# Turning x and k by VectorE blocks over DRAM in a Performer layer's keys pass, with one block of value sums per group

## The reference

```python
xn = _layernorm(x)
q, k, v = xn @ wq, xn @ wk, xn @ wv            # 16 heads of 32
def phi(u):                                    # u scaled by 32 ** -0.25, omega 128 x 32
    proj = u @ omega.T
    return exp(proj - 0.5 * sum(u * u) - max(proj)) / sqrt(128) + 1e-6
kv = einsum('bhsm,bhsk->bhmk', phi(k), v)      # sum over the 1024 rows of a batch
z  = sum(phi(k), axis=rows)
```

## Time and profile before

| | |
|---|---|
| median of 3 runs | 3278.48 us (3276.39 to 3280.28) |
| profiled execution, its own time | 3278.06 us |
| its span, first to last instruction | 3276.3 us |
| PE / PEld / DVE / ACT / POOL busy | 98% / 86% / 69% / 51% / 33% |
| mean granted TensorE clock | 0.992 |
| DMA queue of the kernel | 438.46 MB, 42.2% of 16 engines |

### The profile page before, as it was taken

One profiled execution on the slowest core, in us unless ns is written; L12 is line 12 of the kernel. 1 busy time (PEld: TensorE's weight loads), 2 busy tenths in 40 slices (PEclk: granted clock), 3 DMA queues, 4 the chain that ended last, 5 costly groups with the idle time before them and its releaser, 6 DMA issues.

```text
span 3276.3 us, 73388 instructions
## 1 busy us (share of the span) xinstructions
PE 3213.0 (98%) x28265; PEld 2818.2 (86%) x28265; DVE 2259.3 (69%) x4742; ACT 1656.6 (51%) x3552; POOL 1087.9 (33%) x857
## 2 busy tenths in 40 slices
PE   7999999999899999999999999999999999999998
PEld 6777777777777778787878789999999999999998
DVE  6777777776666666666666666666666766676666
ACT  5666666666545545455545454434444444444443
POOL 3554555554456656565656430000000000000000
PEclk9999999999899999999999999999999999999999
DMA  3222222222444444535444574544554454444443
GB/s 123 94 85 78 101 88 88 95 89 78 119 122 137 128 134 119 149 104 154 118 135 128 158 233 159 166 163 162 168 163 161 154 168 164 151 154 162 163 163 134
DMA packets 314123, 443.16 MB, mean 135 GB/s; under 512 B 162608, under 2 KB 187696, under 8 KB 313776
## 3 DMA queue, kind: packets, MB, share of 16 engines
q1 hardware_dynamic: 313776, 438.46, 42.2%
HBM read 309.28 MB, written 129.11 MB: 134 GB/s over the span
## 4 chain that ended last, share of the span: by engine, by line
PE 45%; POOL 9%; DVE 7%; issue 4%; DMA 4%; ACT 3%; SPq 2%; DVEq 0%; ACTq 0%; POOLq 0%
PE ffn_hidden L189 21%; PE attend_gated L189 13%; PE ffn_result L189 5%; POOL shared_y L1172 3%; PE attend_feat L1335 2%; POOL shared_y L1170 2%; POOL attend_oT_lo L1154 2%; DMA ffn_r_in<-r_d 2%; PE attend_num L1373 2%; PE attend_turn L1373 2%; DVE ffn_yb L1794 2%; POOL attend_ka_lo L1150 1%; ACT ffn_ht_hi L1697 1%; POOL shared_mix_lo L1146 1%; SPq L142 1%
## 5 line engine op out<-in xcount | busy, mean ns | idle before, releaser
L189 PE MATMUL ffn_hidden<-ffn_yT_hi,ffn_wa_hi 128*128 128x256 f32 x2048 | 573.2, 280 | 7.3 <-DVE ffn_wa_lo L1715 4.7
L189 PE MATMUL ffn_hidden<-ffn_yT_lo,ffn_wa_hi 128*128 128x256 f32 x2048 | 574.1, 280 | 0.0
L189 PE MATMUL ffn_hidden<-ffn_yT_hi,ffn_wa_lo 128*128 128x256 f32 x2048 | 572.8, 280 | 0.0
L334 POOL TENSOR_TENSOR ffn_n_rstd<-ffn_n_base,ffn_n_power 128x2 f32<-128x2 f32 x32 | 27.5, 859 | 1277.3 <-DVE ffn_n_negmean L329 1277.3
L189 PEld LDWEIGHTS ffn_hidden<-ffn_yT_hi,ffn_wa_hi 128*128 128x128 f32 x2048 | 386.1, 189 | 8.8 <-DVE ffn_wa_lo L1715 5.6
L189 PEld LDWEIGHTS ffn_hidden<-ffn_yT_hi,ffn_wa_lo 128*128 128x128 f32 x2048 | 386.3, 189 | 0.0
L189 PEld LDWEIGHTS ffn_hidden<-ffn_yT_lo,ffn_wa_hi 128*128 128x128 f32 x2048 | 385.9, 188 | 0.2
L1697 ACT ACTIVATE ffn_ht_hi<-ffn_hs 128x512 fp32r<-128x512 f32 x248 | 156.3, 630 | 431.6 <-DVE ffn_hs L1744 431.6
L1748 DVE TENSOR_TENSOR ffn_ht_lo<-ffn_hs,ffn_ht_hi 128x512 fp32r<-128x512 f32 x248 | 173.6, 700 | 218.7 <-ACT ffn_ht_hi L1697 218.7
L703 ACT ACTIVATE keys_e<-keys_feat,keys_below 128x128 f32<-128x128 f32 x1024 | 282.6, 412 | 55.2 <-DVE keys_below L768 55.2
L638 POOL TENSOR_TENSOR keys_z_sum<-keys_z_sum,keys_e 128x512 f32<-128x512 f32 x192 | 243.7, 1286 | 190.1 <-ACT keys_e L703 190.0
(11 more groups left out here) (281 smaller groups left out, 9406.8 us busy)
## 6 DMA issues: line engine op xcount, KB each, us to landing
ffn_tq<-part_d SPq DMA_DIRECT2D x248, 512.0 KB, 5.3
keys_xin<-in_L_attn_x_dram SPq DMA_DIRECT2D x32, 512.0 KB, 4.2
xn_d<-keys_xn SPq DMA_DIRECT2D x32, 512.0 KB, 2.8
xT_d<-keys_xT_whole SPq DMA_DIRECT2D x32, 512.0 KB, 2.6
u_d<-keys_uq_turned SPq DMA_DIRECT2D x32, 512.0 KB, 2.9
shared_xTf<-xT_d SPq DMA_DIRECT2D x32, 512.0 KB, 6.5
r_d<-shared_gate SPq DMA_DIRECT2D x32, 512.0 KB, 2.8
attend_o<-rden_d SPq DMA_DIRECT2D x128, 128.0 KB, 2.7
```

The costliest lines, as they stand in the source:

```text
L189: last = pe.matmul(out, stationary[a], moving[b], start=start and n == 0, stop=stop and n == len(TERMS) - 1)
```

## The change

Rows are now dealt to partitions in pairs (row 2p + t on partition p), so that a turned group can be put together in row order. xn and k are turned by VectorE in 32x32 blocks, stored to DRAM (`xt_d`, `kt_d`) and loaded back by `load_turned`, four DMAs that put each block where it belongs; xT is loaded whole, rounded and split from SBUF, and stored from there, without GpSimd. Only group 0 is still turned by TensorE (`first`). Products of all three kinds, and the features, read every second column of what was turned (`tile_of`). The floor is no longer added to the exponentials: VectorE sums v over the rows (`v_sum`), and the fold adds the floor times that sum in a further product. The value sums of a group are one job of 64 matmul instructions into one bank (`sums`), added by one VectorE instruction, and it stands right before the second feature block. The pipeline is one group deeper for x: `stats`, `norm` and `turn_x` run three groups ahead, `split` two. Banks, waits, the head and the end lists follow from that.

```diff
-        PE_BODY = [("kv", 0, -1), ("turn_x", 1, 1), ("kv", 1, -1), ("proj", 0, 0), ("k", 0, 1), ("k", 1, 1),
-                   ("kv", 2, -1), ("q", 0, 1), ("proj", 1, 0), ("turn_k", 0, 1), ("kv", 3, -1), ("q", 1, 1),
-                   ("turn_k", 1, 1), ("v", 0, 1), ("fold", 0, -1), ("turn_x", 0, 2), ("v", 1, 1)]
+        PE_BODY = [("k", 0, 1), ("k", 1, 1), ("proj", 0, 0), ("q", 0, 1), ("q", 1, 1), ("v", 0, 1), ("kv", 0, -1),
+                   ("proj", 1, 0), ("fold", 0, -1), ("v", 1, 1)]
+        DVE_BODY = [("v_sum", 1, 0), ("sq_q", 0, 0), ("sq_q", 1, 0), ("turn_k", 0, 1), ("turn_k", 1, 1),
+                    ("top", 0, 0), ("sq", 0, 1), ("stats", 0, 3), ("split", 0, 2), ("split", 1, 2),
+                    ("kv", 0, -1), ("top", 1, 0), ("sq", 1, 1), ("v_sum", 0, 1), ("turn_q", 0, 1), ("turn_q", 1, 1), ("turn_x", 0, 3)]
+        ACT_BODY = [("k", 0, 1), ("k", 1, 1), ("exp", 0, 0), ("exp", 1, 0), ("exp", 2, 0), ("exp", 3, 0),
+                    ("split", 0, 2), ("split", 1, 2), ("q", 0, 1), ("q", 1, 1), ("norm", 0, 3), ("v_out", 0, 1),
+                    ("fold", 0, -1), ("exp", 4, 0), ("exp", 5, 0), ("exp", 6, 0), ("exp", 7, 0), ("v_out", 1, 1)]
+        POOL_BODY = [("z", 0, 0), ("z", 1, 0), ("stats", 0, 3), ("z", 2, 0), ("z", 3, 0), ("z", 4, 0), ("z", 5, 0),
+                     ("z", 6, 0), ("z", 7, 0)]
+        SP_BODY = [("u", 0, 0), ("xt_in", 0, 2), ("kt_out", 0, 1), ("kt_in", 0, 1), ("whole", 0, 2), ("sums", 0, -1),
+                   ("x", 0, 4), ("xn", 0, 3), ("xt_out", 0, 3)]
...
+                if job == "xt_in":
+                    sp.wait_ge(xt_stored, 16 * g + 16)
+                    wait(sp, x_split, 2 * (g - 1))
+                    if g > 1:
+                        wait_alone(sp, xT_stored, 16 * (g - 1), sp_passed)
+                    load_turned(sp, xT_whole[g % 2], xt_d[g], xt_loaded[g % 2])
+                if job == "kt_in":
+                    wait_alone(sp, kt_stored, 16 * g + 16, sp_passed)
+                    for j in range(HC):
+                        wait(sp, feat[j].full, TG * (g - 1))
+                    load_turned(sp, kT[g % 2], kt_d[g], k_loaded[g % 2])
...
+                if job == "split":
+                    act.wait_ge(xt_loaded[g % 2], 64 * (g // 2 + 1))
+                    for t in range(TG):
                         wait(act, v_full[t], g - 1)
+                    act.activation(xT[g % 2].hi[:, 2 * n:2 * n + 2, :], xT_whole[g % 2][:, 2 * n:2 * n + 2, :], ACT.Copy)\
+                        .then_inc(xT_hi, 1)
...
+                if job == "split":
+                    dve.wait_ge(xT_hi, 2 * g + n + 1)
+                    dve.tensor_tensor(xT[g % 2].lo[:, 2 * n:2 * n + 2, :], xT_whole[g % 2][:, 2 * n:2 * n + 2, :],
+                                      f32(xT[g % 2].hi[:, 2 * n:2 * n + 2, :]), ALU.subtract).then_inc(x_split, 1)
                 if job == "turn_x":
+                    wait(dve, xt_stored, 16 * g)
+                    for t in range(TG):
+                        dve.wait_ge(xn_ready, TG * g + t + 1)
+                        dve.transpose(xn_turned[:, :, :, t], xn[:, t, :].rearrange("p (b k) -> p b k", k=KD)).then_inc(x_turned, 1)
...
-                if job == "pk":
-                    t, c = n // NC, n % NC
-                    wait(dve, kv_full, NC * (g - 1) + c + 1)
-                    dve.wait_ge(e_ready[t], NC * g + c + 1)
-                    dve.tensor_scalar(pk[t][:, c, :], e[t][:, c, :], FLOOR, None, ALU.add).then_inc(pk_ready[t], 1)
                 if job == "kv":
+                    total = kv_sum[b % 2][:, :, :].rearrange("p c m -> p (c m)")
...
+                    dve.wait_ge(kv_full, g + 1)
+                    wait(dve, kv_added, g)
                     if i == 0:
+                        dve.tensor_copy(total, sums[:, :]).then_inc(kv_added, 1)
                     else:
+                        dve.tensor_tensor(total, sums[:, :], total, ALU.add).then_inc(kv_added, 1)
...
                 if job == "kv":
+                    wait(pe, kv_added, g)
+                    wait(pe, fold_out, pieces_before(g))
...
+                    for c in range(NC):
+                        for t in range(TG):
+                            for j in range(HC):
+                                h = c * HC + j
+                                last = pe.matmul(sums[rows(j), c * M:(c + 1) * M], v[g % 2][:, t, h * KD:(h + 1) * KD],
+                                                 e[t][:, c, j * M:(j + 1) * M], start=c == 0 and t == 0,
+                                                 stop=c == NC - 1 and t == TG - 1)
                     last.then_inc(kv_full, 1)
                 if job == "fold":
...
+                    if g < G - 1:
+                        pe.wait_ge(kv_added, g + 1)
+                        wait(pe, fold_out, pieces_before(g))
...
+                        pe.matmul(out[:, :, 0:KD], floor[:, :],
+                                  v_sum[b % 2][:, c * M:(c + 1) * M].rearrange("p (h k) -> p h k", k=KD),
+                                  start=False, stop=True)
```

More of the change, by code:

```diff
@@ L336, in invert @@
         pool.tensor_tensor(self.shift[:, :], self.negmean[:, :], self.rstd[:, :], ALU.mult).then_inc(self.ready, 1)
[L339 to L347, removed]
@@ L362 @@
[L362 to L369, removed]
+PE_KEYS_END = (("keys", "k", 0, -1), ("keys", "k", 1, -1), ("keys", "proj", 0, -2), ("keys", "q", 0, -1),
+               ("keys", "q", 1, -1), ("keys", "v", 0, -1), ("keys", "kv", 0, -3), ("keys", "proj", 1, -2),
+               ("keys", "fold", 0, -3), ("keys", "v", 1, -1), ("next", "turn", 0, 0), ("next", "turn", 1, 0),
+               ("keys", "kv", 0, -2), ("keys", "proj", 0, -1), ("keys", "fold", 0, -2), ("next", "turn", 2, 0),
+               ("next", "turn", 3, 0), ("next", "turn", 4, 0), ("keys", "proj", 1, -1), ("next", "turn", 5, 0),
+               ("keys", "kv", 0, -1), ("keys", "fold", 0, -1))
@@ new lines @@
+DVE_KEYS_END = (("keys", "v_sum", 1, -2), ("keys", "sq_q", 0, -2), ("keys", "sq_q", 1, -2), ("keys", "turn_k", 0, -1),
+                ("keys", "turn_k", 1, -1), ("keys", "top", 0, -2), ("keys", "sq", 0, -1), ("keys", "kv", 0, -3),
+                ("keys", "top", 1, -2), ("keys", "sq", 1, -1), ("keys", "v_sum", 0, -1), ("keys", "turn_q", 0, -1),
+                ("keys", "turn_q", 1, -1), ("next", "first", 0, 0), ("next", "lo", 0, 0), ("keys", "v_sum", 1, -1),
+                ("next", "lo", 1, 0), ("keys", "kv", 0, -2), ("keys", "sq_q", 0, -1), ("keys", "sq_q", 1, -1),
+                ("keys", "top", 0, -1), ("next", "lo", 2, 0), ("next", "lo", 3, 0), ("next", "lo", 4, 0),
+                ("keys", "top", 1, -1), ("next", "lo", 5, 0), ("next", "mixed", 0, 0), ("keys", "kv", 0, -1),
+                ("next", "lo", 6, 0), ("next", "lo", 7, 0))
@@ L375 @@
[L375 to L381, removed]
[2 rows of a table added]
@@ new lines @@
+                 ("next", "diff", 0, 0), ("next", "mix", 0, 0))
+SP_KEYS_END = (("next", "w", 0, 0), ("next", "w", 1, 0), ("next", "w", 2, 0), ("keys", "u", 0, -2),
+               ("keys", "kt_out", 0, -1), ("keys", "kt_in", 0, -1), ("keys", "sums", 0, -3), ("keys", "u", 0, -1),
+               ("next", "x", 0, 0), ("next", "mu", 0, 0), ("next", "w", 3, 0), ("next", "w", 4, 0),
+               ("keys", "sums", 0, -2), ("next", "w", 5, 0), ("next", "w", 6, 0), ("next", "q", 0, 0),
+               ("next", "w", 7, 0), ("keys", "sums", 0, -1))
@@ L406, in keys_pass @@
         xT = [Pair(mem, ctx, f"xT{n}", [P, NC, GT]) for n in range(2)]
-        xT_whole = sb("xT_whole", [P, NC, GT])
+        xT_whole = [sb(f"xT_whole{n}", [P, NC, GT]) for n in range(2)]
+        xn_turned = sb("xn_turned", [P, H, KD, TG])
+        uk_turned = sb("uk_turned", [P, H, KD, TG])
         uq = sb("uq", [P, TG, D])
@@ L413, in keys_pass @@
         squares = [sb(f"squares{t}", [P, D]) for t in range(TG)]
-        kT = sb("kT", [P, NC, GT])
+        kT = [sb(f"kT{n}", [P, NC, GT]) for n in range(2)]
         v = [sb(f"v_parts{n}", [P, TG, D]) for n in range(2)]
@@ L419, in keys_pass @@
         e = [sb(f"e{t}", [P, NC, HC * M]) for t in range(TG)]
-        pk = [sb(f"pk{t}", [P, NC, HC * M]) for t in range(TG)]
         kv_sum = [sb(f"kv_sum{n}", [P, NC, M]) for n in range(2)]
+        v_sum = [sb(f"v_sum{n}", [P, D]) for n in range(2)]
         z_sum = sb("z_sum", [P, NC, HC * M])
@@ L424, in keys_pass @@
         fold_z = sb("fold_z", [P, M])
+        floor = sb("floor", [P, M])
         kv_out = sb("kv_out", [P, H, KW])
@@ L492, in pieces_before, with first_bank @@
             return max(0, g - GB + 1)
-        def kv_bank(g, n):
-            return (ring[0], ring[2])[n % 2] if g >= G - 2 else (ring[0], ring[2], ring[1], ring[0])[n]
         def fold_bank(g, c):
-            return feat[c].t if g == G - 1 else turn if g >= G - 3 else ring[0]
-        def turn_of(g, n):
-            return ring[0] if g == 0 and n == 1 else turn
+            return feat[c].t if g == G - 1 else sums
+        def first_bank(n):
```

(5 more changed lines are left out.)

244 lines of the change are left out of this document (102 added, 142 removed), and 17 rows, old and new, of tables (DVE_BODY, DVE_KEYS_END, KEYS_OVER, POOL_KEYS_END).

## The result

The changed kernel took 3526.94 us (median, 3524.9 to 3527.83) against 3277.43 beside it: ratio 1.076 [1.0741, 1.0778]. The forecast, 3223, had the sign wrong. Four readings of the new trace, in the order in which the prediction began.

The account below looks back on a forecast made before the run. TensorE's list was taken as the bound, 24.82 us a group. Bodies -46.8, start -14.5 and end +6 sum to -55.3 us against the median of 3278.48: forecast 3223 us, 8-in-10 range 3199 to 3259.

Parts of the forecast that it names:

- Features to exponentials to features: Each body's loop over TensorE, VectorE and ScalarE: claimed hidden, both ends keeping 2.4 us or more.
- The list: TensorE's work per group with a fold: gains and costs sum to -2.23 us, leaving 22.6 us as floor.
- the joined value block: Four value blocks on TensorE become one of 64 matmuls: 1.89 instead of 2.36 us, gain 0.47; the block lasts 1.96.
- the feature blocks: TensorE's features read every second column: 1.16 us a block against 1.10, +0.12 a body.
- the removed transposes: Sixteen transposes per group leave TensorE: -1.93 us.
- The fold's wait: TensorE's fold waits for VectorE's addition of the value block just ended: 0.4 us a body taken, 0 to 1.3.
- the prediction's upper case: Both split subtractions on VectorE each wait for one GpSimd instruction, so the fold waits 1.3 us.
- The lower clock: No body term; at the pass's end, a feature block noted at 2.09 instead of 1.16 us after TensorE idled.
- X's trip: X goes to DRAM and back before ScalarE rounds it: claimed hidden, at the margin, rows arriving between 11.9 and 15.2.
- rival 2: Slower: x's DRAM round trip becomes the path through ScalarE's rounding; a body takes 27.8 us, about 3364 us; chance 0.09.
- Start and end: Outside the 26 bodies: start -14.5 us (-18 to -9), end +6 us (-2 to +12).
- the slower side: Chance that the changed kernel measures slower than before: 0.09.

Follow-up runs that it names:

- Experiments 1 and 3: Changed kernel with the value block moved right behind the first features: 3245.18 us; changed kernel in its own order with exponential tiles doubled by group parity: 3243.05 us.
- experiment 2: Changed kernel with the value block right behind the first features and VectorE's addition of it ahead of the split subtractions: 3227.85 us, 0.9851 of the original.
- experiments 5 and 6: Changed kernel with VectorE's addition ahead of the split subtractions: 3458.72 us; the same with twelve v products repeated in TensorE's wait: 3369.66 us.

## Why the prediction was wrong

- **The failed step** is "Features to exponentials to features: ... maxima from 7.5, exponentials from 10.3 to 14.6; features 1 want them at 17.2 ... so this loop stays hidden". It followed data forward alone: maxima, exponentials, features. The maxima came in time; the exponentials came at +17.5, because a removed line (`pk`, priced as work that VectorE loses) had let ScalarE write `e` again before TensorE read the copy. I asked of each removed instruction what it cost and not whose buffer it freed. Experiments 1 and 3 show it from two sides.
- **The list** was right: 22.6 forecast, 22.72 measured with TensorE never idle (experiment 2), so the price of the list as a whole is shown. Of its terms, the joined value block (1.95 against 1.96) and the feature blocks (1.16 from start to start, 684.66 to 685.82) came as forecast; the others, the removed transposes among them, were not measured singly.
- **The fold's wait**, 0.4 within 0 to 1.3, is 0.48 on average where the exponentials are free (experiment 1 against 2): 0.71 in three bodies of four, with subtractions of some 1.7 us beside GpSimd's additions, as the prediction's upper case had it, and none in the fourth. In the changed kernel it is 2.60, because the exponentials push everything on ScalarE's queue behind the block.
- **The lower clock** was no term at all for the body, though the prediction had read the price of it at the pass's end (2.09 instead of 1.16). It is 3.45 us of a body (experiments 5 and 6).
- **X's trip** (rival 2) is not the path. SP's timeline and the loads' line, changed kernel:

```profile
682.52 2.60 SPq L141 DMA_DIRECT2D keys_xT_whole<-xt_d  x4
...
DMA to landing us min/median/max: 2.4/3.4/7.4
...
  ACT keys_xT_hi L685: 6.5, 2
```

  The four loads were issued at 682.52, at most 2.6 us to issue and 7.4 to land, and ScalarE asked for the result at 700.5; it waited for loads twice in the whole kernel, 6.5 us. In experiment 2, with the DMA share at 0.61, TensorE waited for nothing.
- **Start and end** were sized wrongly in the good body too: in experiment 2 group 5 starts 8.2 us earlier than before (126.97 against 135.17), not 14.5, and the end is 14.5 longer, not 6. What the start lacks lies in its first two bodies, 46.9 us (15.91 to 62.80) where the prediction's count leaves some 36; the next three take the list's 21.4 each, without a fold. The end was the order of its lists: reordered, it is 1.7 shorter than before.
- Rival 2 had the right sign by chance, with another mechanism and at a third of the price (87 us of 249.5). That the slower side was given 0.09 followed from the same omission: no rival asked about a buffer.

## What to carry to other kernels

A copy that is taken out may have been a second buffer. For every tile that a change lets another engine read directly, ask who writes it next and where the last reader stands on its queue; if reader and next writer's consumer stand side by side on one engine, the wait is in every body. And price a wait on TensorE with its clock: here 4.5 us of idling cost 3.45 more, and a body filled with useless work beat an idle one, once no second wait stood behind the first.

## What was not expected of the hardware

- Some 9 us at half clock behind a wait of 4.5 us (0.50 from 701 to 709), with a busy list ahead and behind; where the fold waited 2.3 us more, nearly 12 (666.88 to 678.7).
- One contention set a rhythm of four bodies (31.5, then three of 33.7 to 34.0), by whether GpSimd copied or added just then; this is read from the rows, as no run changes what GpSimd does.
